# GpSimd's wait for the landing of the preceding chunk, moved behind the first transfer of the new chunk, in a four-layer graph network

## What is computed

```python
# layer 0: an MLP on each edge, summed by destination
h = relu(concat([x[dst], x[src], edge_attr]) @ W1 + b1)
out = segment_sum(h @ W2 + b2, dst)
# layer 1: degree-normalised neighbour sum by destination
agg = segment_sum(x[src] * ci[src][:, None], dst) * cj[:, None]
out = relu(where(in_deg > 0, agg, x) @ W.T + b)
# layer 2: the other way round, summed by source
agg = segment_sum(norm[:, None] * x[dst], src)
out = relu(agg @ W.T + b)
# layer 3: gated messages, summed by source
gate = silu(edge_attr @ W1.T + b1) @ W2.T + b2 + adapt_logit
agg = segment_sum(gate * x[dst] * (cw * mj)[:, None], src) / tot
out = layernorm(x + agg) * gamma + beta
```

## Time and profile before

| what | value |
|---|---|
| median of 3 runs | 20238.29 us (20211.77 to 20250.66) |
| the profiled execution | 20236.51 us |
| its span | 20234.7 us |
| PE busy | 11419.2 us (56%), 63600 instructions |
| PEld busy | 9543.6 us (47%) |
| DVE busy | 9780.5 us (48%), 26342 instructions |
| ACT busy | 3891.4 us (19%) |
| POOL busy | 11133.6 us (55%), 11410 instructions |

### The profile page before, as it was taken

How to read it: one execution, slowest core, us unless ns; L and a number is a source line. 1 busy time by engine, 2 the same in 40 slices (tenths; PEclk the granted TensorE clock), 3 DMA queues, 4 the chain that set the end, 5 groups by cost and what they waited for, 6 DMA issues and landing times. The chain is left out here.

```text
span 20234.7 us, 302760 instructions
## 1 busy us (share of the span) xinstructions
PE 11419.2 (56%) x63600; PEld 9543.6 (47%) x63601; DVE 9780.5 (48%) x26342; ACT 3891.4 (19%) x10412; POOL 11133.6 (55%) x11410
## 2 busy tenths in 40 slices
PE   6666666666656666665666545554464334555545
PEld 5555555555534444343444444444453224444445
DVE  3555555555566666664111455555442225555556
ACT  1000000000122122222333111111122222333331
POOL 4555555555544454444555556666635666666663
PEclk9999999999966666665555555555555555555555
DMA  4333333333211111112333222222222222222222
GB/s 110 77 76 76 76 76 77 77 77 77 67 40 38 39 41 42 41 41 64 90 91 90 78 69 69 70 70 68 64 70 82 77 80 73 75 76 76 76 75 52
DMA packets 1574947, 1407.00 MB, mean 70 GB/s; under 512 B 982792, under 2 KB 1441691, under 8 KB 1570446
## 3 DMA queue, kind: packets, MB, share of 16 engines
q1 hardware_dynamic: 597320, 636.63, 12.3%
q0 software_dynamic: 410000, 462.80, 9.7%
q10 hardware_dynamic: 567508, 306.27, 5.6%
HBM read 984.46 MB, written 420.15 MB: 69 GB/s over the span
## 5 line engine op out<-in xcount | busy, mean ns | idle before, releaser
L1752 POOL DMA_INDIRECT order<-l_msg,l_uring x6250 | 6081.7, 973 | 4212.9 <-DMA order<-l_msg,l_uring 2071.4
L1895 PE MATMUL ps<-l_ordb,l_ohs 128*128 128x49 f32 x15040 | 3307.2, 414 | 2680.7 <-DVE acc L1795 1365.9
L1895 PEld LDWEIGHTS ps<-l_ordb,l_ohs 128*128 128x128 f32 x15040 | 3240.4, 332 | 2747.3 <-DVE acc L1795 1406.5
L548 POOL DMA_INDIRECT l_rows<-btab,l_sd x3125 | 3024.2, 968 | 2368.4 <-DMA l_rows<-btab,l_sd 1388.8
L1088 POOL DMA_INDIRECT l_rows<-y,l_sd x1875 | 1822.2, 972 | 1960.5 <-DMA l_sd<-in_sd 907.1
L1795 DVE TENSOR_TENSOR acc<-acc,ps 128x49 f32 x7520 | 1526.0, 206 | 2158.8 <-issue 1031.0
L689 PE MATMUL ps<-l_rhs,l_lhs 64*128 x6250 | 1455.8, 426 | 824.5 <-DVE l_rows L625 506.5
L689 PEld LDWEIGHTS ps<-l_rhs,l_lhs 64*128 64x128 f32 x6250 | 1358.7, 327 | 911.7 <-issue 910.2
L704 PE MATMUL ps<-l_ohe,l_hid 128*128 128x32 f32 x6250 | 1384.7, 402 | 606.4 <-ACT l_hid L734 606.4
L704 PEld LDWEIGHTS ps<-l_ohe,l_hid 128*128 128x128 f32 x6250 | 1351.8, 331 | 656.7 <-ACT l_hid L734 622.6
L1929 PE MATMUL ps<-l_win,l_oht 96*128 x6250 | 533.1, 241 | 1901.5 <-DVE l_oht L1817 876.6
(11 more groups left out here) (313 smaller groups left out, 14535.0 us busy)
## 6 DMA issues: line engine op xcount, KB each, us to landing
l_ordb<-order SPq DMA_DIRECT2D x752, 250.0 KB
l_dstb<-ids SPq DMA_DIRECT2D x250, 600.0 KB
order<-l_msg,l_uring POOLq DMA_INDIRECT x6250
order<-l_zero ACTq DMA_DIRECT2D x125, 775.0 KB
l_eat<-in_ea40P SPq DMA_DIRECT2D x625, 120.0 KB
gates<-l_made ACTq DMA_DIRECT2D x625, 120.0 KB
l_gin<-gates SPq DMA_DIRECT2D x125, 600.0 KB
l_rows<-btab,l_sd POOLq DMA_INDIRECT x3125
```

The lines of the kernel that those rows point to most:

```text
L548: pool.indirect_dma_start(rows[:, t, :], None, d["btab"], bass.IndirectOffsetOnAxis(ap=sd[:, t, 0:1], axis=0)).then_inc(gat[c], 16)
L1752: pool.indirect_dma_start(d["order"], bass.IndirectOffsetOnAxis(ap=uring[:, t:t + 1], axis=0), msg[:, t, :], None).then_inc(sc[c], 16)
L1895: done = t.matmul(red[b % 2][:, k * MW:(k + 1) * MW], ohs[b][:, k, :], ordb[b][:, k, 0:MW], start=True, stop=True)
```

## The change

The wait for the preceding chunk stands inside the loop over a chunk's tiles, ahead of its second transfer, in place of ahead of the first. The same edit is made in the three functions that issue the transfers of the four layers. All other waits stay ahead of the first transfer.

```diff
@@ pass0 @@
                     pool.nop(nofuse=True)
-                    if c:
-                        pool.wait_ge(gat[c - 1], (g + 1) * 16 * CT)
-                        pool.nop(nofuse=True)
                     for t in range(c * CT, (c + 1) * CT):
+                        if c and t == c * CT + 1:
+                            pool.wait_ge(gat[c - 1], (g + 1) * 16 * CT)
+                            pool.nop(nofuse=True)
                         pool.indirect_dma_start(rows[:, t, :], None, d["btab"], bass.IndirectOffsetOnAxis(
                             ap=sd[:, t, 0:1], axis=0)).then_inc(gat[c], 16)
@@ scatter_pass, layers 2 and 3 @@
-                    if c:
-                        pool.wait_ge(sc[c - 1], (g + 1) * 16 * CT)
-                        pool.nop(nofuse=True)
                     for t in range(c * CT, (c + 1) * CT):
+                        if c and t == c * CT + 1:
+                            pool.wait_ge(sc[c - 1], (g + 1) * 16 * CT)
+                            pool.nop(nofuse=True)
                         pool.indirect_dma_start(d["order"], bass.IndirectOffsetOnAxis(ap=uring[:, t:t + 1], axis=0),
                                                 msg[:, t, :], None).then_inc(sc[c], 16)
```

## The result

The changed kernel takes 22,502.4 us (median of 4 runs, 22,471 to 22,564); the kernel before took 20,244.5 (20,212 to 20,257) beside it. The ratio is 1.112, 95% interval 1.110 to 1.114: slower by 2258 us, where 1518 us less were forecast. The profiled execution spans 22,561.7 us.

The account below looks back on a forecast made before the run. GpSimd's chain of transfers and landing waits was taken to bound most stretches. Savings of 630 + 15 + 40 + 427 + 5 + 70 + 328 = 1515 us gave 18,720 us, range 18,450 to 19,270.

Parts of the forecast that it names:

- What bounds: GpSimd's own chain of transfers and landing waits sets the pace in layer 0 and the last 84 groups of layers 2 and 3.
- The reserve of 3.4 to 4.5 us: Layer 3, last 84 groups: VectorE's first product is ready that early, so 3.9 us a group is saved, 328 us.
- Saved, 1.26 us a boundary: At each layer 0 chunk boundary the first transfer fills 1.26 of the 2.35 us wait; 500 boundaries give 630 us.
- The 3.81 us: Layer 0: landing wait at a boundary after ten transfers in a row, against 2.35 elsewhere; it saves as much, not more.
- VectorE's own loop: Layer 2, last 84 groups: VectorE needs 31.7 us a group, GpSimd 34.8, so the full 427 us is saved.
- The nearest reserve is the 19.2 us above: Layer 0: ScalarE stores a buffer 19.2 us before GpSimd overwrites it, against a gain of 5.0 us a group.
- Layer 1, 0: Two boundaries a group, hidden behind GpSimd's 7.32 us wait for indices, save 0; without that cover 315 us.
- Layer 2's groups with jobs, 15 + 40: Layer 2, groups 1 to 41: first three save 15 us, the rest 40, within 0 to 141 depending on PE's 10.49 us wait.
- Layer 3's first 9 groups, 5: Layer 3's first 9 groups, like layer 2's with jobs: 5 us saved in the first, then 0.
- Layer 3's groups 10 to 41, 70: Layer 3's next 32 groups: 70 us saved, the middle of 0 to 141, depending on ScalarE's unexplained 4.41 us wait.
- the one that ended slower: Rival, chance 0.03: longer streams land late, 3.81 us after the first new transfer, costing 551 us in layer 0; 20,790 us.
- The reading stretches are taken over: Rival, chance 0.12: VectorE's and ScalarE's chains lengthen in the 168 reading groups, which yield 2 us each; 19,270 us.

Follow-up runs that it names:

- e5: Changed kernel plus scratch fills that GpSimd waits for ahead of each chunk but a group's first, idle about 1.8 us; 19,716.5 us, ratio 0.976.
- e8: e5 with three fills in layer 0, layer 1 as in the kernel before, fills ahead of every chunk in layer 2's job groups; 19,333.7 us, ratio 0.954.
- e3: Kernel before with the landing wait kept at even chunks only, giving runs of 10 to 15 transfers; 21,173 us, ratio 1.046.
- e7: Kernel before with one more landing wait at the end of each of layer 2's first 40 groups; 20,046 us, ratio 0.9928.
- m1: Separate measurement without the kernel's work: GpSimd's runs of 25 transfers, with various pauses, beside other engines' independent loops; queues fell to 0.6 to 0.8 instructions a us.
- e1: Changed kernel with 60 empty GpSimd instructions ahead of each chunk's first transfer but a group's first; 23,521 us, ratio 1.159.

## Why the prediction was wrong

- **What bounds**: right for layer 0 and for layer 2's last groups; a shorter pause (e5, e8) made both faster (41.8 to 38.5 and 37.9, 39.9 to 38.2 and 38.0). Not shown for layer 3's last 84 groups: with the same shorter pause they stayed at 39.3 and 39.2, and at 26 of their 84 starts GpSimd then stood some 4 us for ScalarE. The reserve of 3.4 to 4.5 us there was smaller than read.
- **Saved, 1.26 us a boundary**: right for GpSimd. The idle stretches were 0.30 and 1.09, 0.30 and 0.71, where 0.30 and 1.1, 0.30 and 0.7 were forecast. The landings came when they had come (0.30 + 0.95 + 1.09 is 2.34, before 2.35). The Trainium skill's page "DMA: Bandwidth & Descriptors", section "Latency and other measured facts", says that access to the large memory takes longer under high load, and by that rule the waits would have grown. They did not, and the loss was not there; but the load was not higher either, 74 GB/s in layer 0 for 76 and 55 for 69 in layer 2's reading stretch, so the rule itself stays untested.
- **The 3.81 us "where ten transfers went out in a row"**: the ten are not the reason. In e3 the runs of ten and more in layer 0 ended with landing waits of 2.4 us on average, those in layer 2 with 2.1. What makes the wait long at a group's second chunk is not shown.
- **The step that failed**: the reserves of the other engines ("VectorE's own loop is 39.9 less the waits of 1.83 and 6.42, 31.7 us, below the 34.8 that POOL would need", and "The nearest reserve is the 19.2 us above"). They were worked out with the others' pace in the kernel before, as if it didn't depend on what GpSimd does. It does: its pauses are when they catch up. In layer 2's reading stretch a group takes 49.9 us now, not 34.8; with the 1.8 us pause it takes 38.2. Layer 3's reading stretch, forecast 328 us shorter, is 745 longer, and layer 0, forecast 630 shorter, is 197 longer.
- **Layer 1, 0**: wrong for the same reason. GpSimd had idle time there, so nothing was gained, but the gathers of a group now run as a stream of 15, and the group takes 2.7 us more. The cover named, the wait for the indices, grew from 907 to 1531 us in all.
- **Layer 2's groups with jobs, 15 + 40**: 25 us were gained. The 10.49 us of PE ended with GpSimd's run of ten, for which the trace gave "only a coincidence". It may be more: with a wait at that run's end (e7) the group fell by 4.2 us. The cause is not shown.
- **Layer 3's first 9 groups, 5**: +73 instead.
- **Layer 3's groups 10 to 41, 70**: +140 instead. With fills they fell to 38.7 us, so ScalarE's 4.41 us didn't hold them at 40.8. What its unnamed releaser is stays open.
- **The rivals**: the one that ended slower named the right sign and the wrong mechanism (late landings), at 0.03. "The reading stretches are taken over" named the right engines, but saw closer packing as the reason and still left a gain of 2 us a group; it was a loss of 10.1 and 8.9.

The warning stood in the trace before, not in a wait but in the queues' own instructions: SP's register instructions were long in 12% to 26% of cases on the third to fifth transfer of a run in layer 2's reading groups, and never on the first. I had read waits and operations, which don't show it.

What the resource is that a stream holds up, these runs can't tell. They show what it does to each queue, that plain transfers of GpSimd's don't do it, and that a pause is shared.

## What to carry to other kernels

A wait of GpSimd between bursts of indirect transfers may be doing work for every other engine. Before it is hidden, compare the duration of the other queues' register instructions inside a burst and behind a pause; where they jump from 40 to 700 ns, start with a pause of 1.5 to 2 us per five transfers, which served here, and try its length and spacing stage by stage. A reserve read from one trace holds only as long as the engine's pace does; a stretch with idle time everywhere and "issue" as the releaser is a sign that it no longer does.

## What the runs showed of the hardware

- In an unbroken stream of indirect transfers (0.95 us each, 0.30 between) VectorE, ScalarE, PE and SP fall from between 2 and 10 queue instructions a us (2 for ScalarE, 5 for PE, 7 to 8 for VectorE, 8 to 10 for SP in m1) to 0.6 to 0.8 each. Beside each other VectorE and ScalarE had their first long instruction after 28 to 49 others; VectorE alone kept up for 9.2 us and 122 instructions, ScalarE alone for 12 us and about 100. Beside 25 plain transfers of GpSimd's (0.54 us each) none fell.
- Per 25 scatters VectorE did 47, 66, 82, 142, 153 and 187 operations at idle stretches of 0.3, 1.1, 1.3, 1.8, 2.0 and 3.2 us after every five.
- Sixty empty instructions on GpSimd's queue made no pause: its 0.30 us between transfers stayed as they were (e1).
